# The row that DVE compares with moves from SBUF into a PSUM bank; three step banks instead of four

## The reference, cut to what matters

```
h   = layernorm(x)
agg = segment_sum(h[src], dst) / max(degree, 1)
x   = x + concat(h, agg) @ W.T + b                 # graph layer
z   = layernorm(x)
y   = sum over the 2 best of 8 experts of weight * (gelu(xn(z) @ W1[e] + b1[e]) @ W2[e] + b2[e])
out = x + y                                        # mixture of experts
```

## Time and profile before

| | us |
|---|---|
| median of 3 runs | 1563.37 |
| lowest, highest | 1557.92, 1567.36 |
| profiled execution, whole time | 1560.88 |
| its span, first to last instruction | 1558.0 |
| busy in the span: PE, DVE, ACT, POOL | 1190.0, 773.3, 491.0, 1119.2 |
| mean granted TensorE clock (share of full speed) | 0.864 |

### The profile page before, as it was taken

The page is one execution under the profiler, slowest core; times in us unless marked ns, Lnnn a source line. Parts: engine busy times, 40 slices in busy tenths (PEclk is TensorE's granted clock), DMA queues, the critical chain, the costliest instruction groups (busy, mean ns, idle before and its releaser), DMA issues.

```text
span 1558.0 us, 22055 instructions
## 1 busy us (share of the span) xinstructions
PE 1190.0 (76%) x5524; PEld 902.0 (58%) x5524; DVE 773.3 (50%) x2574; ACT 491.0 (32%) x1094; POOL 1119.2 (72%) x1049
## 2 busy tenths in 40 slices
PE   3376886978587877986888588778888687787992
PEld 1154353655366754764677376547766576675892
DVE  9544365546345463464447353634646364654320
ACT  3300040321033421432244134313333334334771
POOL 3577777777777777777777777777777777774333
PEclk9976887987688996998889798978999898898996
DMA  8966554443344444444444444445445445445332
GB/s 265 313 210 190 161 183 125 121 116 110 119 130 126 118 115 121 122 112 130 120 114 126 112 121 124 109 115 136 120 119 133 109 116 132 117 118 135 68 62 34
DMA packets 128442, 203.62 MB, mean 131 GB/s; under 512 B 23484, under 2 KB 95988, under 8 KB 128192
## 3 DMA queue, kind: packets, MB, share of 16 engines
q0 software_dynamic: 60336, 136.52, 34.5%
q1 hardware_dynamic: 64452, 64.36, 13.5%
q10 hardware_dynamic: 3532, 1.34, 0.3%
HBM read 153.66 MB, written 49.27 MB: 130 GB/s over the span
## 4 chain that ended last, share of the span: by engine, by line
PE 44%; POOL 15%; DMA 15%; issue 10%; DVE 9%; ACT 5%; DVEq 1%; ACTq 0%; SPq 0%; POOLq 0%
PE psum L632 14%; DMA work<-h_rows,srcs 11%; PE psum L725 11%; POOL work L560 10%; PE psum L700 9%; PE psum L645 4%; POOL queue L569 3%; DMA out_dram<-expert_buf,tok_idx 3%; DVE acc L945 2%; POOL out_dram L580 2%; PE psum L679 1%; ACT expert_buf L531 1%; PE psum L646 1%; ACT region L467 1%; PE psum L656 1%
## 5 line engine op out<-in xcount | busy, mean ns | idle before, releaser
L560 POOL DMA_INDIRECT work<-h_rows,srcs x830 | 826.5, 996 | 264.9 <-issue 181.9
L632 PE MATMUL psum<-work 128*128 128x257 f32 x1660 | 567.3, 459 | 198.3 <-DMA work<-h_rows,srcs 170.6
L945 DVE TENSOR_TENSOR acc<-acc,psum 128x257 f32 x830 | 350.5, 422 | 584.1 <-PE psum L632 530.4
L632 PEld LDWEIGHTS psum<-work 128*128 128x128 f32 x1660 | 321.5, 221 | 340.9 <-DMA work<-h_rows,srcs 249.9
L580 POOL DMA_INDIRECT out_dram<-expert_buf,tok_idx x105 | 173.2, 1649 | 112.5 <-DMA out_dram<-expert_buf,tok_idx 58.0
L725 PE MATMUL psum<-region,expert_buf 128*128 x840 | 229.4, 422 | 18.4 <-ACT expert_buf L525 14.0
L531 ACT ACTIVATE expert_buf<-psum,b_col 128x128 f32<-128x128 f32 x420 | 120.0, 369 | 328.8 <-PE psum L700 320.4
L700 PE MATMUL psum<-expert_buf 128*128 128x128 f32 x1680 | 208.9, 278 | 2.7 <-ACT expert_buf L523 2.6
L700 PEld LDWEIGHTS psum<-expert_buf 128*128 128x128 f32 x1680 | 204.5, 194 | 10.4 <-ACT expert_buf L523 3.3
L725 PEld LDWEIGHTS psum<-region,expert_buf 128*128 128x128 f32 x840 | 173.2, 214 | 57.0 <-issue 31.6
L838 DVE TENSOR_TENSOR work<-iota,rel 128x1152 f32<-128x1152 f32 x98 | 126.9, 1295 | 55.0 <-PE psum L632 29.1
(11 more groups left out here) (193 smaller groups left out, 783.8 us busy)
## 6 DMA issues: line engine op xcount, KB each, us to landing
expert_buf<-queue SPq DMA_DIRECT2D x105, 130.0 KB
work<-h_rows,srcs POOLq DMA_INDIRECT x830, 2.8
region<-in_L_ffn_W_dram SPq DMA_DIRECT2D x16, 512.0 KB, 5.9
h_rows<-region SPq DMA_DIRECT2D x7, 896.0 KB, 4.3
x_rows<-region SPq DMA_DIRECT2D x7, 896.0 KB, 12.3
own<-h_rows SPq DMA_DIRECT2D x49, 128.0 KB
own<-x_rows SPq DMA_DIRECT2D x49, 128.0 KB
out_dram<-acc SPq DMA_DIRECT2D x49, 128.0 KB, 2.5
```

Source lines behind the costliest of these rows:

```text
L560: pool.indirect_dma_start(grow[:, t % RING, 0:D], None, h_rows, bass.IndirectOffsetOnAxis(srcs[:, t:t + 1], 0)).then_inc(got[t % RING], 16)
L632: summed.up(pe.matmul(STEP_BANKS[t % BANKS][:, 0:GW], hot[:, k, :], grow[:, t % RING, :], start=True, stop=True))
L945: added.up(dve.tensor_tensor(sums, sums, STEP_BANKS[t % BANKS][:, 0:GW], ALU.add))
```

## The change

`iota` is copied once into PSUM bank 7 (COUNT), and the comparison takes its first input from there. The steps have three banks (0 to 2) in place of four; PAIR, ROUTE, TURN and HID move down by one bank. In the tail the results alternate between bank 2 and COUNT. The other uses of `iota` (L856, L894, L898) keep the SBUF copy.

```diff
-    BANKS = 4
+    BANKS = 3
...
-    STEP_BANKS, PAIR, ROUTE, TURN, HID = psum[0:4], psum[4], psum[5], psum[6], psum[7]
+    STEP_BANKS, PAIR, ROUTE, TURN, HID, COUNT = psum[0:3], psum[3], psum[4], psum[5], psum[6], psum[7]
...
-        return TURN[:, D:2 * D] if not in_tail(j) else psum[2 if j % 2 else 3][:, 0:D]
+        return TURN[:, D:2 * D] if not in_tail(j) else result_bank(j)[:, 0:D]
...
-        return TURN if not in_tail(j) else psum[2 if j % 2 else 3]
+        return TURN if not in_tail(j) else psum[2] if j % 2 else COUNT
...
-        hot_up.up(dve.tensor_tensor(hot[:, k0:k0 + n, :], iota[:, :].unsqueeze(1).broadcast_to([P, n, P]),
+        hot_up.up(dve.tensor_tensor(hot[:, k0:k0 + n, :], COUNT[:, 0:P].unsqueeze(1).broadcast_to([P, n, P]),
                                     rel[:, first:first + n].unsqueeze(2).broadcast_to([P, n, P]), ALU.is_equal))
...
         acc_zero.wait(dve)
+        d_own.then(dve.tensor_copy(COUNT[:, 0:P], iota[:, :]))
         one_hot(0, HALF, 0)
```

## The result

| | before | after |
|---|---|---|
| median, us | 1563.31 (4 runs, 1557.92 to 1567.36) | 1524.96 (4 runs, 1523.55 to 1526.30) |
| profiled execution, its span, us | 1560.88, 1558.0 | 1526.30, 1524.8 |
| mean granted TensorE clock (profiled execution) | 0.864 | 0.884 |

The ratio is 0.9757, with a 95% interval of 0.9726 to 0.9788: 38 us, 2.4% faster. Predicted were 1527 us.

The account below looks back on a forecast made before the run. POOL, handing out its 997 DMAs without free time, was taken as the limit. Stalls of 40.8 us, less 4 for banks and 1.5 for the first scatter, gave 35 us off 1560.9 or 1563.4: 1527 us, range 1516 to 1546.

Parts of the forecast that it names:

- POOL is the limit, and the wait for PE is a pause: From 58 to 1408 us POOL has no free time; its waits for PE are 0.305 us pauses between DMAs.
- "no change" to "slower": Whole-kernel outcomes other than faster: same had a chance of 0.07, slower 0.08.
- 77 stalls, 41.9 us, all go: POOL's DMAs started inside DVE's comparisons: with the first input in PSUM all 77 stalls vanish, 41.9 us less on POOL.
- The comparison's own duration, 0: DVE's 98 comparisons reading from PSUM: between 2 us less and 2 us more in all, taken as 0.
- The copy, 0.25 us hidden: One copy of the row into PSUM before the first comparison: 0.25 us, hidden in idle time, cost 0.
- Three banks, 4 us: PE's steps wait for the sum of t-3, not t-4: mostly hidden, 4 us lost after 1217 us.
- rival 3: PE's bursts during DVE's comparisons and lists: banks decide, 0.5 us per block, 74 us less 42, about 1595; chance 0.03.
- The first scatter, 1.5 us: POOL's first scatter, at 235.18 us: with POOL ahead, it waits 1.5 us for its places.
- After the last gather nothing changes: The stretch after the last gather, from 1408 us, 150 us long, keeps its length.
- The sum: Whole kernel: 40.8 - 4 - 1.5 = 35 us gained, predicted time 1527 us.

Follow-up runs that it names:

- experiment 4: Kernel after with one more indirect DMA on POOL at every 32nd step, 26 in all: 1556.81 us, ratio 0.9882 to the kernel before.
- Experiment 3: Kernel after with every eighth step's matrix product made twice on PE, 104 more: 1527.40 us, ratio 0.9702 to the kernel before.
- Experiment 1: Kernel after with three banks, but the comparison takes its row from SBUF again: 1568.38 us, ratio 0.9959 to the kernel before.
- experiment 5: Kernel before, unaltered, run again with its profile on a slower chip: 1804.22 us, ratio 1.0026.
- 8: Kernel before (four banks, row in SBUF) with comparisons cut into pieces of three matrices, on a slower chip: 1823.89 us, ratio 1.0134.
- 9: Kernel before (four banks, row in SBUF) with comparisons cut into pieces of three matrices, on the other slower chip: 1820.39 us, ratio 1.0113.
- experiment 2: Kernel after with two step banks in place of three, row in PSUM: 1528.82 us, ratio 0.9712 to the kernel before.

## Why the prediction was right, step by step

**POOL is the limit, and the wait for PE is a pause.** Right, where the kernel before takes 1563 to 1575 us: POOL's stream is full before and after, and experiment 4 put 32.7 us into POOL and 29 to 33 us came out. Experiment 3 put 104 more products into PE and nothing came out, though PE as a whole was busy only 10.6 us more. The chain of waits says of the kernel after `PE 45%; POOL 13%`, and would still send a reader to PE. On the two other chips the step doesn't hold, and it is the reason why the forecast would have been wrong there: "no change" to "slower", the outcome that had 0.15 of the chance. No row of the first profile hinted at such chips. That the result was measured where POOL is the limit is luck, as far as the forecast is concerned.

**77 stalls, 41.9 us, all go.** Right: no gather is left above 1.01 us, and POOL is busy 41.3 us less. The last gather starts 39.5 us earlier (1406.7 and 1367.2); forecast was 40.8 - 1.5 = 39.3. Experiment 1 brings 39.7 us of stalls back, and its time is 41.0 us above that of experiment 3 beside it. (The 16 gathers inside an L1009 that the forecast went by are those with over 0.15 us of it to run; 24 start inside one in all, and their mean is 0.96 us too.) The inference of the Trainium skill's page "SBUF — State Buffer", section "Who interferes with whom", that descriptor generation is not held by a Vector instruction with two SBUF inputs, doesn't hold for this kernel's gathers: 2116 ns with the row in SBUF, 1008 with it in PSUM, and nothing else changed (experiment 1 and the kernel after). Which part of a gather's issue is held, a read or a write, no run shows.

**The comparison's own duration, 0.** Right. DVE's groups by form, kernel after, to be set against the earlier trace rows:

```profile
L838 DVE TENSOR_TENSOR work<-psum,rel 128x1152 f32<-128x1152 f32 x49 | 66.3, 1353 | 0.0
L838 DVE TENSOR_TENSOR work<-psum,rel 128x1024 f32<-128x1024 f32 x49 | 60.1, 1226 | 54.6 <-issue 27.6 <-PE psum L632 27.0
```

3 and 8 ns less for each, 0.5 us in all. The fixed extra cost for PSUM that the Trainium skill's page "VectorE: DVE Perf Modes" gives in "The TRN2 errata" doesn't show.

**The copy, 0.25 us hidden.** It took 0.294 us, at 57.9 us, before the first comparison; the first gather began at 58.2 as before.

**Three banks, 4 us.** No run shows this cost. Experiment 1, three banks with the row in SBUF, was 6 us faster than the kernel before beside it, and not 4 slower. PE's wait for the additions rose to 45.8 us, as forecast, and its wait for gathers fell to 130.3 (forecast 120 to 140). PE's last step lay 37.0 us earlier, 2.5 less than POOL's last gather. But two banks made PE wait 64 us more for DVE and cost some 4 us. So the slope that rival 3 was built on, 0.5 us for each of some 150 blocks, isn't there; most of it takes the place of PE's other waits.

**The first scatter, 1.5 us.** Right in place, 2.12 us in size, 1.8 of it more than the usual pause.

**"After the last gather nothing changes".** This is the step that was off, by 3.8 us. From the last gather to the end the kernel before takes 151.3 us and the one after 157.6; 2.5 of these 6.3 are PE's lag just named. The windows from the last gather on, kernel before and kernel after (columns as in the earlier trace rows):

```profile
1408.00:1440.00 32.00, 24.57 (x123) 20.74 (x123) 13.17 (x75) 13.76 (x32) 12.23 (x10) 0.84 0.50 130
1440.00:1558.00 118.00, 87.53 (x602) 80.91 (x601) 26.56 (x131) 65.40 (x161) 40.86 (x27) 0.90 0.35 55
```

```profile
1367.00:1405.00 38.00, 29.46 (x126) 23.95 (x125) 14.95 (x82) 16.12 (x37) 13.23 (x11) 0.73 0.46 123
1405.00:1525.00 120.00, 88.12 (x602) 81.03 (x602) 27.26 (x135) 66.88 (x165) 40.86 (x27) 0.90 0.34 55
```

Behind it both need the same. In the first stretch the granted clock was 0.73 and not 0.84: a matmul took 234 ns in the mean (29.46 / 126) and not 200 (24.57 / 123), which over 126 of them makes 4.3 us. The other profiles tell more. From PE's last step to the end it's 144.0 us in the kernel before and 144.7, 144.1 and 144.5 in experiments 1, 2 and 4, but 147.7 and 147.8 in the kernel after and in experiment 3. Here are the 16 us that begin some 4 us after PE's last step, in the kernel after, experiment 3, experiment 2 and experiment 4:

```profile
1381.00:1397.00 16.00, 12.37 (x44) 10.13 (x45) 4.26 (x30) 4.23 (x12) 3.55 (x3) 0.51 0.56 166
```

```profile
1380.00:1396.00 16.00, 12.88 (x46) 10.65 (x47) 4.10 (x27) 3.72 (x10) 4.24 (x4) 0.50 0.64 183
```

```profile
1386.00:1402.00 16.00, 12.00 (x57) 10.01 (x58) 4.73 (x28) 4.31 (x12) 3.55 (x3) 0.79 0.62 167
```

```profile
1416.00:1432.00 16.00, 12.24 (x57) 10.23 (x58) 4.32 (x28) 4.22 (x13) 3.54 (x3) 0.79 0.62 167
```

In the first two the granted clock stays at the lower of its two levels (1.2 GHz, half) nearly through the whole stretch, and PE gets through 44 and 46 matmuls; in the others it comes back to the full one inside it, and PE gets through 57. All four have the row in PSUM, and experiment 4 has three banks as well. So the 3.8 us go with the clock in that stretch, and not with the row or the banks; why it comes back late in two of the profiles is open.

**The sum.** 35 us forecast; between the two spans it's 33.2, between the profiled executions 34.6, between the medians 38.3. Terms: 39.5 on POOL (39.3 forecast), -2.5 until PE's last step and -3.8 in the tail (-4 forecast, for the banks). The large term is right by its mechanism. That the small ones come close together is luck in part: the 4 us taken off stood for banks, and more than half of what was lost is the clock in the tail.

## What to carry to other kernels

Before believing the chain of waits, add up an engine's instructions and the shortest pause between them over the stretch: if that fills it, the engine is the limit, whatever it is said to wait for. Then look at the spread of durations of its commonest instruction, because a few long ones among many equal ones can show contention that no wait names. Measure on more than one chip before a change is kept: what is taken from an engine is worth its full time only where that engine is the limit. And when an engine is given more work to see whether it is the limit, look at its whole busy time and not only at the lines added: in experiment 3 the two differ, 10.6 and 53 us.

## What the runs showed of the hardware

- A gather that POOL starts while DVE is in a comparison with both inputs in SBUF takes until that instruction's end and 0.81 to 0.88 us more (kernel before, experiments 1, 5, 8 and 9); a gather of 0.95 us took up to 1.35 beside pieces of 0.55 us and up to 2.13 beside a comparison of 1.35. One that starts in the comparison's first 0.03 us, or in its last 0.1 us, takes its usual 0.94 to 0.99. With the first input in PSUM none is held: at most 1.01 us in the kernel after.
- Each gather costs POOL's stream a pause of 0.305 us beside its own 0.95 (26 added ones: 24.8 + 7.9 us), and the kernel paid both.
- Three chips ran the kernel before: one at 1574.55 us, two at 1799.03 and 1801.66. Between a profile of 1558.0 us (first measurement) and one of 1805.1 us (experiment 5) the busy times of DVE (773.3 and 774.0 us), ACT (491.0 both) and POOL (1119.2 and 1118.9) are the same. PE is busy 1190.0 and 1238.6 us; the other 198 us are waiting. On the two slower chips the gain of 2.4% was a loss of 1.3 to 1.5%.
- Behind PE's last step the granted clock stayed at 1.2 GHz for 16 us in two profiles (0.51 and 0.50 in the mean) and came back to 2.4 GHz within it in four (0.79); from that step to the end they took 147.7 and 147.8 us, and 144.0 to 144.7.
